# Transformer block with mixture of experts on one core: first weights and stores in another order on the DMA queue, and a new table of shifts for the planner

## What is computed

```python
x = x + attention(layernorm(x))       # causal, softmax over keys
x = x + ffn(layernorm(x))
# attention: Q, K, V = x @ Wq + bq, x @ Wk + bk, x @ Wv + bv
#   h     = gelu(norm(x @ dp_w1 + dp_b1) * ln_g + ln_b)
#   drift = h @ dp_w2 + dp_b2
#   gate  = tanh(gelu(drift * g_w1 + g_b1) @ g_w2 + g_b2)   # one number for each key
#   out   = (softmax(Q K^T / 4) * gate) V, then @ Wo + bo
# ffn: sigmoid router, 2 of 8 experts for each token (silu(x w1) * (x w3)) w2, plus a shared expert
```

## Time and profile before

| | |
|---|---|
| median of 3 runs | 1788.8 us (1788.64 to 1791.04) |
| the profiled execution | 1798.91 us |
| its span in the trace | 1797.1 us |
| mean granted clock of PE | 0.968 of full speed |
| PE busy | 1650.4 us, 92% of the span |
| DVE busy | 1288.9 us, 72% |
| ACT busy | 1079.7 us, 60% |
| POOL busy | 810.5 us, 45% |

### The profile page before, as it was taken

One profiled execution on the slowest core, in us unless ns is written; L12 is line 12 of the kernel. 1 busy time (PEld: TensorE's weight loads), 2 busy tenths in 40 slices (PEclk: granted clock), 3 DMA queues, 4 the chain that ended last, 5 costly groups with the idle time before them and its releaser, 6 DMA issues.

```text
span 1797.1 us, 34689 instructions
## 1 busy us (share of the span) xinstructions
PE 1650.4 (92%) x12770; PEld 979.4 (54%) x12770; DVE 1288.9 (72%) x2550; ACT 1079.7 (60%) x1808; POOL 810.5 (45%) x1390
## 2 busy tenths in 40 slices
PE   7799999889999999899998999999998989989889
PEld 3344455435544665456554566555654556657677
DVE  4777777857796768677696768877696656854666
ACT  3467755555657655675658666675557655657533
POOL 5325532453355221742238762543217674156761
PEclk9699999989999999999999999999999999999999
DMA  5557655544455444454455764534435655336440
GB/s 151 159 161 231 163 173 151 167 140 122 111 150 152 132 119 117 141 142 118 142 148 167 210 178 142 154 112 121 153 104 167 185 165 154 103 111 188 149 129 30
DMA packets 192709, 261.26 MB, mean 145 GB/s; under 512 B 19616, under 2 KB 127264, under 8 KB 192544
## 3 DMA queue, kind: packets, MB, share of 16 engines
q1 hardware_dynamic: 181792, 229.67, 44.3%
q0 software_dynamic: 10752, 29.37, 5.6%
HBM read 130.98 MB, written 127.40 MB: 144 GB/s over the span
## 4 chain that ended last, share of the span: by engine, by line
PE 53%; DVE 13%; ACT 10%; POOL 7%; DMA 7%; issue 5%; SPq 4%; another core or an unknown queue 1%; POOLq 0%; DVEq 0%; ACTq 0%
PE ps_all L2075 10%; PE ps_all L1965 10%; DVE mx L1551 6%; PE ps_all L1945 6%; PE ps_all L1912 6%; PE ps_all L2106 5%; ACT probs L1362 5%; PE ps_all L1896 4%; PE ps_all L1882 3%; PE ps_all L1974 2%; POOL xs_s L1211 2%; DMA qk_s<-ql 2%; PE ps_all L2085 1%; PE ps_all L1997 1%; DMA x<-in_x 1%
## 5 line engine op out<-in xcount | busy, mean ns | idle before, releaser
L1551 DVE TENSOR_REDUCE mx<-ps_all 128x2 f32<-128x1024 f32 (+2 forms) x640 | 620.6, 1005 | 157.1 <-PE ps_all L1912 84.2
L1362 ACT ACTIVATE probs<-ps_all 128x1024 f32<-128x1024 f32 x576 | 572.3, 1027 | 194.3 <-PE ps_all L1945 176.4
L1179 POOL TENSOR_SCALAR_AFFINE_SELECT probs<-probs 128x256 f32<-128x256 f32 (+1 forms) x448 | 190.8, 443 | 534.2 <-ACT probs L1362 529.9
L1965 PE MATMUL ps_all<-probs,vaug 128*32 128x512 f32 (+3 forms) x3072 | 323.0, 517 | 29.4 <-POOL probs L1179 18.9
L1912 PE MATMUL ps_all<-k_st,q_st 63*128 63x512 f32 (+3 forms) x1536 | 267.3, 399 | 41.0 <-ACT probs L1362 14.5
L1945 PE MATMUL ps_all<-q_st,k_st 64*128 64x512 f32 (+3 forms) x1536 | 262.3, 401 | 26.8 <-ACT probs L1362 11.8
L1912 PEld LDWEIGHTS ps_all<-k_st,q_st 63*128 63x128 f32 x1536 | 133.2, 190 | 162.7 <-issue 53.3
L1945 PEld LDWEIGHTS ps_all<-q_st,k_st 64*128 64x128 f32 x1536 | 128.9, 191 | 148.7 <-issue 65.6
L2075 PE MATMUL ps_all<-w_hi,x2h 128*128 128x512 f32 (+1 forms) x480 | 169.9, 354 | 3.2 <-DVE x2l L1600 2.2
L1808 DVE SCALAR_TENSOR_TENSOR act_t<-act_t,ps_all 128x256 f32<-128x256 f32 x168 | 70.2, 419 | 133.2 <-ACT act_t L1423 125.6
L1423 ACT ACTIVATE act_t<-ps_all 128x256 f32<-128x256 f32 x168 | 64.5, 385 | 161.3 <-PE ps_all L2075 116.4
(11 more groups left out here) (197 smaller groups left out, 2831.3 us busy)
## 6 DMA issues: line engine op xcount, KB each, us to landing
qk_s<-qh SPq DMA_DIRECT2D x116, 256.0 KB
q_st<-qk_s SPq DMA_DIRECT2D x128, 192.0 KB
k_st<-qk_s SPq DMA_DIRECT2D x128, 192.0 KB
xs<-xs_s SPq DMA_DIRECT2D x72, 256.0 KB
ys_s<-ysb SPq DMA_DIRECT2D x72, 256.0 KB
o_s<-o_sb SPq DMA_DIRECT2D x64, 256.0 KB
qk_s<-ql SPq DMA_DIRECT2D x57, 256.0 KB
xs_s<-ysb SPq DMA_DIRECT2D x20, 512.0 KB, 6.2
```

Source lines behind the costliest of these rows:

```text
L1179: last = nc.gpsimd.affine_select(out=block, in_=block, compare_op=ALU.is_ge, fill=0.0, base=0, pattern=[[0, heads], [1, P]], channel_multi ...
L1362: nc.scalar.activation(to, of, ACT.Exp, scale=DH ** -0.5).then_inc(freed[release[item][0]], 1)
L1551: last = nc.vector.tensor_reduce(to[:, :, p, qt % QPC], both[:, :, at:at + keys], X_AXIS, ALU.max)
L1965: last = mm(bank(first)[32 * h:32 * h + 32, q0 - c * CHUNK:], vaug[:, kt, g, h * VW:h * VW + 32], probs[:, s % 2, h, at:at + cols], start= ...
```

## The change

`load_weights` issues Wq, Wk and bqk in its first step and Wv, dp_w1 and their biases in its second; AQ needs the first step in the plan, AV the second. WC may be planned from 15.9 instead of 14 us and is given 4.8 instead of 3.4 us. Batch 0 has new due times for WL, AV, AQ and the gate; `FIRST` goes from 50 to 42 us. The x of batch 1 may be planned from 36 instead of 70 us (`EARLY_X`), the later stores of batch 0 from 36 instead of 48 us (`EARLY_SQ`). `SAME_TILING` goes from 14000 to 12000, and nearly all entries of `LATER` are new. `HOLD` is 0 and does nothing. What is computed doesn't change.

```diff
-SAME_TILING = 14000
+SAME_TILING = 12000
...
-FIRST = 50_000
+HOLD = 0
+EARLY_X, EARLY_SQ = 36_000, 36_000
+FIRST = 42_000
...
-LATER = {"AB": 8000, "AC": 15000, "AE": 22000, "AG": -1000, "AN": 4000, "AQ": -1000, "AR": -5000, "AS": -1000,
+LATER = {"AB": 21000, "AC": 18000, "AE": 25000, "AG": 10000, "AN": 7000, "AQ": -1000, "AR": 5000, "AS": -13000,
...
-            due = begin + (end - begin) * h / HALVES
+            step = (end - begin) / HALVES
+            due = begin + step * h if n else -30_000 + 1_000 * h
...
-                lands=5500 if n else 2600, early=70_000 if n == 1 else 0)
+                lands=5500 if n else 2600, early=EARLY_X if n == 1 else 0)
...
-                    due_q = due + (end - begin) / HALVES * 0.25 * v - 60_000 * (n == 0 and v < 2)
+                    due_q = due + step * 0.25 * v if n else (500 * v - 40_000 if v < 2 else step * (h + 0.5 * v))
                     add("PE", ("AQ", n, c, v), 1716, due_q,
-                        [("WL", 1)] + [("AC", n, t) for t in range(c * QPC, (c + 1) * QPC)] + before, 1, FULL)
+                        [("WL", 0)] + [("AC", n, t) for t in range(c * QPC, (c + 1) * QPC)] + before, 1, FULL)
...
-                    due_v = due + (end - begin) / HALVES * (0.5 + 0.12 * (t - c * QPC)) - 40_000 * (n == 0 and c)
-                    add("PE", ("AV", n, t), 1290, due_v, [("WL", 0), ("AC", n, t), ("VA", n - 1, GROUPS - 1)], 1, FULL)
+                    due_v = due + step * (0.5 + 0.12 * (t - c * QPC)) if n else 1_000 * t - 25_000
+                    add("PE", ("AV", n, t), 1290, due_v, [("WL", 1), ("AC", n, t), ("VA", n - 1, GROUPS - 1)], 1, FULL)
...
-                add("SP", ("SQ", n, c, v), 3 * ISSUE, due, [("QL", n, c, v)], lands=3600, early=48_000 if v > 1 else 0)
+                add("SP", ("SQ", n, c, v), 3 * ISSUE, due, [("QL", n, c, v)], lands=3600, early=EARLY_SQ if v > 1 else 0)
...
-        due = at(n) - T * (0.3 if n else 0.05)
+        due = at(n) - T * 0.3 if n else -10_000
...
-        add("SP", ("WC",), 3400, 14000, lands=4000, early=14000)
+        add("SP", ("WC",), 4800, 14000, lands=4000, early=15900)
...
                 if k == 0:
+                    for w, name in ((wq, "Wq"), (wk, "Wk")):
+                        sp.dma_start(w[:], ins[name].rearrange("(k p) n -> p k n", p=P)).then_inc(wqk_in, 16)
+                    sp.dma_start(bqk[:], ins["bqk"]).then_inc(wqk_in, 16)
+                else:
                     sp.dma_start(wvd[:, :, 0:E], ins["Wv"].rearrange("(k p) n -> p k n", p=P)).then_inc(wv_in, 16)
...
-                else:
-                    for w, name in ((wq, "Wq"), (wk, "Wk")):
...
```

More of the change, by code:

```diff
@@ L425, in maxima @@
                 blocks = len(qts) * (1 if p is not None else PAIRS)
-                due = begin + GROUP_T * 0.9 * u / NMAX
+                due = begin + GROUP_T * 0.9 * u / NMAX + HOLD * (gi == 0 and c > 0)
                 add("PE", ("M", n, g, u), 240 if kc < c else 310 if blocks == 1 else 445, due,
@@ L920, in load_weights @@
                     sp.dma_start(vd_bias[:, E:], row("dp_b1", 0, DP)).then_inc(wv_in, 16)
-                else:
-                    for w, name in ((wq, "Wq"), (wk, "Wk")):
-                        sp.dma_start(w[:], ins[name].rearrange("(k p) n -> p k n", p=P)).then_inc(wqk_in, 16)
-                    sp.dma_start(bqk[:], ins["bqk"]).then_inc(wqk_in, 16)
             def load_constants(item):
```

## The result

| | before | after |
|---|---|---|
| median of 12 runs | 1787.14 us | 1767.22 us |
| all runs | 1774.64 to 1791.04 | 1756.14 to 1777.1 |
| ratio | | 0.9888, 95% interval 0.9869 to 0.9907 |
| profiled execution, its span | 1798.91, 1797.1 | 1770.53, 1768.7 |
| granted clock, mean | 0.968 | 0.972 |

The change makes the kernel 1.1% faster, 20 us. The forecast was 1782.8 with a range from 1772 to 1793. Lines of the changed kernel are four higher than those of before.

What follows compares the result with a forecast made beforehand. PE was taken as the bound, busy 92%, standing still most at batch 0's attention start. Terms -3.6 - 1 + 0 - 3 + 1.6 + 0 = -6.0 us gave 1782.8 us, range 1772 to 1793.

Steps and rivals of the forecast that it cites:

- The rest: All other moved work, waits for POOL's masks included: 0, from -7 to +7 us, as no instruction is added or taken.
- Fillers: 59 fewer zero multiplications on PE, mostly in idle time: -3 us, ends 0 and -12.7.
- Front: First stores at the kernel's start: key store sooner, chunk 1's stores landed 3.6 us sooner; -3.6 us, ends 0 and -5.
- everything later hangs on this: Claim that all later work depends on PE's waits for chunks 0 and 1, 2.84 and 7.03 us, at the start.
- The wait at the first values: Start of the kernel: PE newly waits 1.2 us for the last DMA the first values need, now issued later.
- Earlier x of batch 1: 80 to 92 us: batch 1's turns and projections fill some PE idle time; -1 us, between 0 and -1.9.
- Gate's table loads: Batch 0's gate: two table loads of 1.28 us each go; term 0, between -2.6 and +2 us.
- Tilings: 20 more tiling changes on PE at 0.08 us each: +1.6 us, ends 0 and +3.
- Rival 1: Front gain eaten by chunk 1, whose maxima start at 53 us as before: 1786.4 us, no change; chance 0.16.
- Rival 2: New order really tighter: all 59 fillers count and the 381 us stall goes; 1773, or 1766 us; chance 0.18.
- Rival 3: Slower by the clock: with fewer fillers PE idles more in attention and clocks lower; three more stretches give 1796 us; chance 0.10.
- Rival 4: Slower by one or two more 7 us waits for POOL's scatters: 1790 to 1797 us; chance 0.06.

Runs made afterwards that it cites:

- e9: Splice: the order of before up to batch 7's first transpose of the maxima, the changed order after it; ratio 0.9878 to the kernel before.
- e15: Splice: changed order up to the first transpose of the maxima of batch 7's third group of heads, then the order of before; ratio 0.9961 to before.
- e1: The kernel before with all 120 fillers left out, order untouched; ratio 1.0022 to the kernel before, 1767.3 us.
- e2: The changed kernel with its 61 fillers left out, order untouched; ratio 0.9943 to the kernel before, 1754.7 us.
- e3: The kernel before with only the new front (q and k weights first, constants behind the first key store); ratio 1.0004 to the kernel before.
- e4: The changed kernel with the front undone (old weights first, constants back ahead of the key store); ratio 0.9902 to the kernel before.
- e10: Splice: the changed order up to batch 7's first transpose of the maxima, the order of before after it; ratio 1.0035 to the kernel before.
- e16: The changed kernel with 121 fillers in place of 61, order untouched; ratio 0.9903 to the kernel before.
- e5: The changed kernel unchanged, run again as a control in another group of runs; ratio 0.9870 to the kernel before.
- e8: The changed kernel with the old table of shifts (`LATER`), its other changes kept; ratio 1.0147 to the kernel before.
- e7: The kernel before with the new table of shifts (`LATER`) alone; ratio 1.0151 to the kernel before.

## Why the prediction was wrong

- **The rest, 0, from -7 to +7.** This is the step that failed. The prediction read the first 92 us and the longest wait, at 381 us, and gave the remaining 1700 us of a new order one symmetric term of 0, with no other reason than that no instruction was added or taken. The runs show -12.7 us for the order without fillers, and all of it in batch 7's attention and behind it (e9 to e15): 9 to 12 us in batch 7 where the clock stays up, some 9 behind its last maxima. The stall of 6.96 us did go (the longest wait for POOL's masks is 2.5 us after): at the transpose of the maxima behind it, near 410 us, the new order is 6.6, 4.2 and 5.9 us ahead (before and after, e1 and e2, e3 and e4). But this isn't kept: at batch 7 the same pairs are 5.2, -5.1 and 2.5 us apart, and e10 is 0.15 to 0.56% slower than before.
- **Fillers, -3.** The size is neither shown nor refuted. The reasoning that most of them stood in waits was right (19 us of work for 22 us of waits, e1), but the step to "nearer to 0" left out what they give back by the clock: taking out all 120 makes the kernel before 0.2% slower, taking out all 61 the changed one 0.5 to 0.7%. The nearest test of the term is e16, with 60 more on the changed kernel: 0.9903 against 0.9888 and 0.9870, so slower by 3 to 6 us at most and perhaps not at all. The end of -12.7 fails, by e1.
- **Front, -3.6.** The term failed, in two steps. The third DMA of the key store, forecast at 21.4, went at 22.95: issue took 2.0 us more than in the queue of before. And chunk 1's last store, taken as landed 3.6 us sooner, was issued 3.3 us sooner and landed 0.6 sooner. Beyond that, "everything later hangs on this" was wrong: in e3 the run on DVE does begin 1.4 us sooner than in e1, and at 219 us nothing of it is left. e3 puts weights and constants at 0 (-3 to +4 us).
- **The wait at the first values, 1.2:** 0.71 measured. **Earlier x of batch 1, -1:** PE has 1.09 us more in 80 to 92 us. **Gate's table loads, 0:** two are gone (one of 16 here, one of 8 at line 1328). No run isolates these three; all the changed order ahead of batch 7 together brings nothing (e10).
- **Tilings, +1.6:** no run isolates it. It is smaller than what a ratio here can tell.
- **The range.** The ends of the terms, added up, go from -29 to +12, so from 1760 to 1801. The prediction took 1778 to 1787 for them without saying how, and 1772 to 1793 in all; the measured 1767.2 lies within its own ends.
- **Rival 1** had the front's case, and a slower landing behind another store among its causes; it was right on the front and wrong on the total.
- **Rival 2** was right in its name, that the new order is tighter, and had 0.18. That its 1766 is next to the measured 1767.2 is luck: 12.7 us of it for 59 fillers is refuted by e1, and the 7 for the stall aren't kept.
- **Rival 3** (clock) did not decide. Its mechanism is real: without fillers the mean clock is 0.968 and 0.969, against 0.977. But the changed kernel with its 61 lost next to nothing by it: 0.972 against 0.968 in the profiled pair, 0.975 against 0.976 in the group of e5. **Rival 4** (a scatter stall again) did not come.

What stays open: which moves make batch 7's first groups shorter. There PE's work, waits and clock all improve a little, and no single wait stands out.

## What to carry to other kernels

Here the new order was worth something only in the last round and behind it, where other work runs out. So read the end of the trace as closely as the start, and ask which independent work is left to cover the last serial steps. A change to the front of a long pipeline should be followed to the place where it would be cashed in; here chunk 1's last store was issued 3.3 us sooner, its first use came 0.75 us sooner, and e3 has nothing of such a gain left at 219 us. And when an order is changed as a whole, a splice of the old and the new at a mark tells in two kernels where the gain lies, while taking back single parameters of the planner told nothing but that none of them has the gain alone. The fillers that such a splice moves along have to be counted, or left out as in e1 and e2.

## What the runs showed that I had not expected

- Issue of DMAs stretches when stores stand close: the first two DMAs of the key store took 2.57 to 2.89 us of SP's queue right behind another store (after, e2, e3, e5, e8), and 1.23 to 1.85 behind the constants (before, e1, e4, e7).
- Issuing a store sooner hardly let it land sooner. Chunk 1's last one, of 256 KB, was issued at 33.45 to 37.33 us in the first five and landed at 44.5 to 45.5; in the other four it was issued at 39.00 to 39.60 and landed at 45.7 to 46.1. Its way took 7.2 to 11.3 us in the former and 6.1 to 6.8 in the latter. The cause isn't shown.
- Multiplications by zeros in the waits pay, up to a point: the clock's mean is 0.968 without and 0.977 with 120 of them (before), and in the changed kernel 0.969 without, 0.973 and 0.975 with 61 (after, e5), and 0.978 with 121, which gave no time over 61.
- The same kernel on the same chip had medians of 1762.5 and 1783.4 us in two groups of runs, at nearly the same mean clock (0.977 and 0.976). A difference of 1% between groups says nothing; only ratios within a group were used.
